# Four more gather slots and eight more one-hot slots in the first attention of a graph network, with the residual rows kept in DRAM meanwhile

## What is computed

```python
def gat_conv(x, W, attn_l, attn_r, src, dst, n_nodes):      # first attention: H = 8 heads, D = 64
    H, D = attn_l.shape
    feat = (x @ W).reshape(n_nodes, H, D)
    el = jnp.einsum('nhd,hd->nh', feat, attn_l)
    er = jnp.einsum('nhd,hd->nh', feat, attn_r)
    e = jax.nn.leaky_relu(el[src] + er[dst], NEG_SLOPE)
    m = jax.ops.segment_max(e, dst, num_segments=n_nodes)
    ex = jnp.exp(e - m[dst])
    denom = jax.ops.segment_sum(ex, dst, num_segments=n_nodes)
    alpha = ex / denom[dst]
    out = jax.ops.segment_sum(alpha[:, :, None] * feat[src], dst, num_segments=n_nodes)
    return out.reshape(n_nodes, H * D)

x = gat_conv(x, W1, attn_l1, attn_r1, src, dst, n)
x = jax.nn.elu(x)
out = gat_conv(x, W2, attn_l2, attn_r2, src, dst, n)
```

## Time and profile before

| | us |
|---|---|
| median of 3 runs | 3238.77 |
| lowest and highest | 3231.11, 3247.51 |
| the profiled execution | 3237.48 |
| its span in the trace | 3235.5 |
| first attention, slots with lookups (1489 to 2055) | 566 |
| first attention, slots alone (2087 to 2756) | 669 |

### The profile page before, as it was taken

One profiled execution on the slowest core, in us unless ns is written; L12 is line 12 of the kernel. 1 busy time (PEld: TensorE's weight loads), 2 busy tenths in 40 slices (PEclk: granted clock), 3 DMA queues, 4 the chain that ended last, 5 costly groups with the idle time before them and its releaser, 6 DMA issues.

```text
span 3235.5 us, 50165 instructions
## 1 busy us (share of the span) xinstructions
PE 2677.7 (83%) x18059; PEld 2018.5 (62%) x18059; DVE 2259.8 (70%) x3543; ACT 748.7 (23%) x1529; POOL 1001.8 (31%) x1234
## 2 busy tenths in 40 slices
PE   4777777999899998886888898477787777876999
PEld 3666665545455555775777776365566556674888
DVE  7999997897334444987676777655555555785786
ACT  7888884020001112000000000400000000403443
POOL 3000000111102223005665666466666666003000
PEclk8999999999899999997999999788888888967999
DMA  4444446433477773216676676466766666061553
GB/s 135 184 182 167 184 165 251 125 113 129 135 254 263 257 248 127 61 51 186 191 194 179 185 198 170 118 188 183 190 185 185 185 186 192 24 198 55 159 162 109
DMA packets 311084, 538.11 MB, mean 166 GB/s; under 512 B 108482, under 2 KB 213460, under 8 KB 310596
## 3 DMA queue, kind: packets, MB, share of 16 engines
q1 hardware_dynamic: 241700, 309.63, 29.1%
q0 software_dynamic: 69152, 225.28, 24.9%
HBM read 420.89 MB, written 115.11 MB: 166 GB/s over the span
## 4 chain that ended last, share of the span: by engine, by line
PE 46%; DVE 30%; POOL 8%; issue 6%; another core or an unknown queue 5%; ACT 3%; DMA 2%; DVEq 0%; SPq 0%; ACTq 0%; POOLq 0%
PE ps L1513 14%; PE ps L1744 11%; PE ps L1720 8%; DVE a L592 8%; PE ps L1649 5%; POOL a L1854 4%; DVE a L587 3%; POOL wts L1854 3%; DVE a L588 3%; PE ps L1417 2%; DVE a L1179 2%; DVE a L848 2%; DVE wts L1179 2%; PE ps L1647 1%
## 5 line engine op out<-in xcount | busy, mean ns | idle before, releaser
L1854 POOL DMA_INDIRECT a<-t,mid x502 | 488.8, 974 | 443.9 <-DVE cin L958 167.8
L1513 PE MATMUL ps<-a 128*128 128x512 f32 x1200 | 556.4, 603 | 13.3 <-DVE a L781 13.3
L1744 PE MATMUL ps<-wts,a 128*128 128x260 f32 x1312 | 356.6, 423 | 100.5 <-issue 58.9
L1744 PE MATMUL ps<-a,oh 128*128 128x260 f32 x1344 | 365.5, 424 | 65.0 <-issue 56.5
L1480 PE MATMUL ps<-a 128*128 128x200 bf16 x1568 | 319.1, 255 | 109.4 <-issue 50.4
L1179 DVE TENSOR_TENSOR a<-a,ps 128x1040 f32<-128x1040 f32 x251 | 309.9, 1235 | 126.9 <-DMA a<-t,mid 114.4
L1854 POOL DMA_INDIRECT wts<-t,mid x328 | 315.8, 963 | 214.9 <-issue 81.3
L1744 PEld LDWEIGHTS ps<-wts,a 128*128 128x128 f32 x1312 | 274.4, 213 | 165.9 <-issue 120.4
L1744 PEld LDWEIGHTS ps<-a,oh 128*128 128x128 f32 x1344 | 280.8, 212 | 131.0 <-issue 84.3
L1513 PEld LDWEIGHTS ps<-a 128*128 128x128 f32 x1200 | 219.2, 192 | 221.4 <-issue 214.9
L1804 POOL TENSOR_SCALAR rstd<-mv 128x1 f32<-128x1 f32 x75 | 30.3, 404 | 916.7 <-DVE mv L479 914.5
(11 more groups left out here) (337 smaller groups left out, 4100.3 us busy)
## 6 DMA issues: line engine op xcount, KB each, us to landing
a<-at_d SPq DMA_DIRECT2D x60, 1280.0 KB, 6.2
at_d<-a SPq DMA_DIRECT2D x49, 800.0 KB, 3.3
mt_d<-a SPq DMA_DIRECT2D x49, 800.0 KB, 4.9
a<-mt_d SPq DMA_DIRECT2D x30, 1280.0 KB, 6.2
a<-trlo_d SPq DMA_DIRECT2D x49, 512.0 KB
ot_d<-a SPq DMA_DIRECT2D x49, 320.0 KB, 5.5
a<-ot_d SPq DMA_DIRECT2D x49, 256.0 KB, 3.6
a<-t,mid POOLq DMA_INDIRECT x502
```

What stands on the lines that cost most here:

```text
L1513: m = e.matmul(acc[f].rearrange("p (x d) -> p x d", x=8), X[:, hi, P * f:P * (f + 1)], a, start=(hi == 0), stop=end, skip_group_check=True)
L1744: t = e.matmul(ps[:, 512 * u:512 * u + 2048][:, bass.ds(c, 260)], ohs[so][:, k, :], hrows[2 * r + k][:, 260 * u:260 * (u + 1)], start=Fals ...
L1854: e.indirect_dma_start(out=hrows[2 * r + k], out_offset=None, in_=t2, in_offset=bass.IndirectOffsetOnAxis(ap=srci[:, k, s:s + 1], axis=0)) ...
```

## The change

NR goes from 10 to 14 and RO from 10 to 18. The place for the four slots of rows and the eight of one-hots is `xres`, whose 6400 floats a partition are copied to a DRAM tensor `x_d` before and read back after. SP issues the copy out behind the two loads from `h_d` and ahead of the table loads, DVE and POOL wait for it (`xd_out`) before slot 0 and before the first gather; SP issues the copy back when PE has finished the last slot, and DVE waits for it (`xd_in`) in the second attention. DVE makes the one-hots of slot s + 1 before it waits for the rows of slot s, and its product waits for the one-hots of its own slot. PE no longer waits for `head_oh`, and takes the limit of `acc_ready` at even slots only, that of the odd slot behind.

```diff
-NR = 10
+NR = 14
-RO = 10
+RO = 18
...
+        x_d = dram("x_d", [P, NB * D])
...
+        xresf = xres[:, :, :].rearrange("p b n -> p (b n)")
...
+        hpair += [xresf[:, 2 * W1 * i:2 * W1 * (i + 1)] for i in range(NR - 10)]
...
-        ohs = [oh[:, i, :, :] for i in range(4)] + [a4[:, 544 + 256 * i:800 + 256 * i].rearrange("p (k n) -> p k n", k=2) for i in range(RO - 4)]
+        ohs = [oh[:, i, :, :] for i in range(4)] + [a4[:, 544 + 256 * i:800 + 256 * i].rearrange("p (k n) -> p k n", k=2) for i in range(6)]
+        ohs += [xresf[:, 8 * W1 + 256 * i:8 * W1 + 256 * (i + 1)].rearrange("p (k n) -> p k n", k=2) for i in range(RO - 10)]
...
             e.wait_ge(*V.last())
+            e.wait_ge(xd_out, 16)
 
             for s in range(NS):
-                r, so = s % NR, s % RO
-                if s >= RO:
-                    e.wait_ge(head_mm, s - RO + 1)
-                for k in range(2):
-                    e.tensor_scalar(ohs[so][:, k, :], iota[:, :], ndl[:, k, s:s + 1], None, ALU.is_equal).then_inc(head_oh, 1)
+                r = s % NR
+                for i in range(0 if s == 0 else s + 1, min(s + 2, NS)):
+                    if i >= RO:
+                        e.wait_ge(head_mm, i - RO + 1)
+                    for k in range(2):
+                        e.tensor_scalar(ohs[i % RO][:, k, :], iota[:, :], ndl[:, k, i:i + 1], None, ALU.is_equal).then_inc(head_oh, 1)
                 e.wait_ge(gh_in[r], 32 * (s // NR + 1))
...
+                e.wait_ge(head_oh, 2 * s + 2)
                 bv = hpair[r].rearrange("p (h d) -> p h d", h=16)
...
-                e.reg_alu(lim, lim_regs[s % 4], 1, ALU.max)
-                e.wait_ge(acc_ready, lim)
-                e.wait_ge(head_oh, 2 * s + 2)
+                if s % 2 == 0:
+                    e.reg_alu(lim, lim_regs[s % 4 + 1], 1, ALU.max)
+                    e.wait_ge(acc_ready, lim)
                 e.wait_ge(head_mul, s + 1)
...
             e.wait_ge(*V("cin", 0))
+            e.wait_ge(xd_out, 16)
             for s in range(NR):
                 gather_heads(s)
...
+            e.wait_ge(act_norm, 2 * NB)
+            e.dma_start(x_d, xresf).then_inc(xd_out, 16)
             for g in range(3, LOOKS_A // 4 + 3):
                 one_hots_back(8, g)
...
             e.wait_ge(head_mm, NS)
+            e.dma_start(xresf, x_d).then_inc(xd_in, 16)
             e.dma_start(msmall, mt_d[NHEX - 1, :, :]).then_inc(msmall_in, 16)
```

More of the change, by code:

```diff
@@ L411, in program @@
         out_done = sem("out_done")
+        xd_out, xd_in = sem("xd_out"), sem("xd_in")
         consts = sem("consts")
@@ L1142, in attention2 @@
                 node_row(6)
+                e.wait_ge(xd_in, 16)
                 for t in range(len(TILES2) + ARG_AHEAD):
```

## The result

The changed kernel takes 3247.78 us (median of 11 runs) beside 3235.82 us of the kernel before (11 runs); the ratio is 1.0046, 95% interval 1.0033 to 1.006. Run again later beside the kernel before it gave 1.0028 (1.0013 to 1.0042). By the ratios it is slower by 15 and 9 us (the medians lie 12.0 and 8.3 us apart), where I had forecast 1.8 us less. Its profiled execution took 3243.62 us, with a span of 3241.8.

A forecast was written before the change was run, and what follows sets the result against it. No engine was taken as full: PE stutters while POOL's gathers run unbroken and recovers when they stop, so a deeper ring gains only once. 3237.5 − 4 + 7 − 2 − 2 = 3236.5, so 3237 us; range 3190 to 3264.

The forecast's parts named there:

- Before slot 0: Start of the first attention: POOL gathers four slots more before PE frees a place; nothing waits for those rows, so 0.
- rival 3: PE's stutter spreads to a quarter of part A as gathers run longer unbroken: 30 us, total 3267; chance .09.
- part A: First attention's stretch with table lookups beside the head products, 566 us; forecast to stay within 10 us of that.
- my three signs of a wrong forecast: POOL's part B stops falling over a third, PE's part A issue idle over 10 us, DVE's spill gap over 15 us.
- The spill, +7: Copy of xres out, before slot 0: the table lands behind it and DVE stands 7 us; bounds 0 to +20.
- Four slots ahead at the end, −4: Where gathers end: last gather 11.8 us earlier, less 7.8 us for four slots PE still runs; bounds 0 to −12.
- part B: First attention's stretch of head products alone, 669 us; forecast to stay within 10 us of that.
- The reload, 0: Copy of xres back after the last slot: 13.5 us of transfer, over before attention 2's first lookup, so 0.
- One-hots −2: First attention: one-hots made a slot ahead spare PE its waits for DVE, −2 us (0 to −6).
- PE's instructions −2: First attention: 207 REGISTER_ALU and some waits fewer on PE, −2 us (0 to −5); 0 if instruction streaming hides them.
- rival 1: The ring holds part B: without POOL's 62 stops 90 us less, 3147, chance .08; a third of it, 3207, chance .21.

The follow-up runs named there:

- the third chip: Chip where the kernel before takes 3024.51 us (21 runs), 6.5% less; four changed kernels ran there, among them the kernel before with 207 fewer REGISTER_ALU: 1.0004.

## Why the prediction was wrong, point by point

- *Before slot 0.* The step that failed. "The same four slots are also gathered before slot 0 ... nothing waits for those rows", priced at 0, is right about the rows and wrong about what gathering them does: +11.5 us (47.1 for 35.6 from first gather to first product). I had read the mechanism out of the earlier trace rows, PE stuttering once gathers have run unbroken for some ten microseconds, and rival 3 asked where else such runs would get longer. It looked at part A alone, and at PE's idle, not at what PE announces. The run that grows for certain, from 20 to 28 gathers, is the one before slot 0, and DVE waited 3.35 us at its end already, for a lookup done 6.3 us before. None of my three signs of a wrong forecast looked there, and none of them came up. With this term the sum would have been 3248, the measured 3247.78, though partly by luck, as the next points show.
- *The spill, +7.* Right in sign, too large: +3.0 in the two profiles, +3 to +5.5 over all of them, in two pieces. The h_d loads take 12.7 to 14.5 us with the copy behind them (11.2 to 11.8 without, 13.4 in one trace), though issued ahead: I had taken their time as fixed. And DVE waits 1.6 us for the table instead of 7. I had put the spill wholly behind the loads; part of it runs beside them, and it lands 20.1 us after its issue, at 1304.67. The table lands 0.8 us later, 21.8 us after the issue of the h_d loads, and not 26.8:

```profile
1288.51 16.96 DMA dst_n<-ot_d
```

- *Four slots ahead at the end, −4.* Confirmed in size: part B takes 3 to 7 us less than with ten (10 on the third chip), and the last run of PE is 91 records. That PE's steady state doesn't depend on the ring held too: as many stops, as much idle.
- *The reload, 0.* Right: 478.8 us from last slot to end with it, 479.4 without.
- *One-hots −2, PE's instructions −2.* Neither shows: 1.0005 and 1.0004. The 0 that I had beside the −2 for the instructions was the better value.
- *Part A.* I read DVE's "remote" waits for lookups as a chain between PE and DVE, and rival 3 took part A as nearly free of the stutter. The third chip, with 100 us less in part A and no "remote" wait, speaks against both. It doesn't change the forecast, since both kernels have it. (In rival 1 the sum of 108.9 is 109.0.)
- *What is open.* The measured pieces give −5 + 11.5 + 4 = +10 us, between the 9 and 15 us of the two measurements; the one pair of profiled executions differs by 6.3. From PE's first product to its wait for ACT, the first four traces with copies are 7 to 11 us shorter than the two without, but later it is the other way round (559 with, 545 without), so I take it as chance. From the last slot to the end the first five kernels with the changed loops take 482 to 485 us against 478 to 482 of those without; the wait of 17.56 us is 19 to 20 us in them and 13 to 21 in the others, and I draw nothing from it. Why one chip holds PE up and another doesn't isn't shown. Nor is it shown for the start that the unbroken run counts, and not the number of gathers under way; only the second attention rules out their bytes.

## What to carry to other kernels

When a ring gets deeper, look first at the place where it is filled from empty: there the longer run of transfers is certain, while in the steady state only the consumer's pace counts. If one engine's idle has no cause in the profile, look for what another engine does during all of it, and then for every other place where the same thing goes on; here the same pattern cost 11 us at the start and 18 us in a stage that nobody had changed. A long "remote" wait is worth a look at when the work waited for was done: here it was done 15 to 17 us before. A pause of POOL at a landing is cheap where its transfers are not urgent (25 small gathers, ratio 0.993) and dear where POOL is the bound (1.03 to 1.14).

## What the runs showed of the hardware

- During a long unbroken run of POOL's indirect DMAs what PE has finished is announced late: 17.4 us for a lookup before slot 0 (record ended 1478.87, counted 1496.27), 15.0 us for the products of the second attention (2936.38, 2951.39), and PE's single records come with 0.3 to 2.5 us between them. It happened with transfers of 512 bytes as with 260 KB.
- Before slot 0 PE's stutter sets in 9 us after the 1.25 us cadence begins (1469.25 to 1478.4 in the kernel before, 1470.69 to 1480.2 in the changed one), and counts are 3 us late from 6 or 7 us on. It ends 2 to 3 us after POOL's last gather; in the second attention the count came when the last DMA but one had begun.
- Pauses of some 2 us after each four DMAs took the wait in the second attention from 17.56 to 3.20 us. Pauses of 0.5 to 2 us at each slot took three quarters of the stutter in part B, pauses of 1 us after each six gathers a quarter.
- It differs from chip to chip, as far as one session on the third can tell: the same program runs 6.5% faster there with nothing of it. The changed kernel as it is was not run there; with ten slots ahead it came out at 0.9987, where another chip has 1.0021.
- Two loads already issued (3.2 MB) take 12.7 to 14.5 us when a store of 3.3 MB is put behind them on the same queue, 11.2 to 11.8 without it (13.4 in one trace).
